# A gather stage with POOL fills in it, selections made for two groups at a time, and fewer waits on PE

## What is computed

```
def _gcn_conv(x, src, dst, ew, W, b, n_nodes):
    xW = x @ W
    deg = jax.ops.segment_sum(ew, dst, num_segments=n_nodes) + 1.0
    dinv = jnp.where(deg > 0, jax.lax.rsqrt(deg), 0.0)
    norm = dinv[src] * ew * dinv[dst]
    agg = jax.ops.segment_sum(norm[:, None] * xW[src], dst, num_segments=n_nodes)
    agg = agg + (dinv * dinv)[:, None] * xW
    return agg + b
...
h1 = jax.nn.relu(_gcn_conv(layernorm(x), ..., W1, b1, n))
h2 = jax.nn.relu(_gcn_conv(h1, ..., W2, b2, n))
x = x + h2
x = x + moe(layernorm(x))
```

## Time and profile before

| | |
|---|---|
| three runs, us | 5221.11, 5225.19, 5214.46 |
| the profiled execution, us | 5177.12, its span 5175.3 |
| first stage, up to POOL's first gather | 427 us |
| layer 1, POOL's first to last gather | 427 to 2677 us |
| layer 2, from POOL's first gather to the end | 2689 to 5175 us |
| busy shares of the span | PE 74%, weight loads 68%, POOL 58%, DVE 44%, ACT 14% |

### The profile page before, as it was taken

How to read it: one execution, slowest core, us unless ns; L and a number is a source line. 1 busy time by engine, 2 the same in 40 slices (tenths; PEclk the granted TensorE clock), 3 DMA queues, 4 the chain that set the end, 5 groups by cost and what they waited for, 6 DMA issues and landing times.

```text
span 5175.3 us, 82233 instructions
## 1 busy us (share of the span) xinstructions
PE 3841.7 (74%) x27222; PEld 3496.5 (68%) x27223; DVE 2298.3 (44%) x8827; ACT 722.4 (14%) x2277; POOL 3003.7 (58%) x3241
## 2 busy tenths in 40 slices
PE   3445565555555555555558999999999999999999
PEld 3424454554555545555557899889989899988998
DVE  6732222222222222222224655566556655656655
ACT  1020000000000000000001222222222222222222
POOL 0104666666666666666666666666666666656663
PEclk9998766766666666667668999999999999999999
DMA  3244333333333333333333333333333333333332
GB/s 95 62 144 122 99 97 97 100 96 98 98 97 100 96 97 99 95 98 98 97 94 93 95 97 99 96 96 96 96 98 96 96 97 98 96 93 95 95 97 59
DMA packets 243540, 500.39 MB, mean 97 GB/s; under 512 B 61453, under 2 KB 141656, under 8 KB 243179
## 3 DMA queue, kind: packets, MB, share of 16 engines
q0 software_dynamic: 150528, 411.24, 28.0%
q1 hardware_dynamic: 87210, 79.56, 4.9%
q10 hardware_dynamic: 5440, 5.01, 0.3%
HBM read 456.90 MB, written 38.67 MB: 96 GB/s over the span
## 4 chain that ended last, share of the span: by engine, by line
PE 28%; DVE 19%; POOL 18%; issue 16%; another core or an unknown queue 14%; DMA 3%; DVEq 2%; SPq 1%; ACT 0%; POOLq 0%; ACTq 0%
POOL msg L461 18%; PE part L736 11%; DVE sel L1047 5%; PE psY L730 5%; PE psH L721 3%; PE psY L736 3%; DVE mix L1175 2%; PE psH L736 2%; DMA msg<-ytab,srcT 1%; DVEq L272 1%; DVE accbuf L1055 1%; DVE accbuf L989 1%; DVE nt L1129 1%; PE psT L689 1%
## 5 line engine op out<-in xcount | busy, mean ns | idle before, releaser
L461 POOL DMA_INDIRECT msg<-ytab,srcT x3136 | 2968.1, 946 | 1878.2 <-issue 962.3
L736 PE MATMUL part<-sel,msg 128*128 128x96 f32 x8384 | 1155.9, 293 | 255.6 <-issue 207.9
L736 PEld LDWEIGHTS part<-sel,msg 128*128 128x128 f32 x8384 | 1113.6, 210 | 310.6 <-issue 270.1
L730 PE MATMUL psY<-w_s,hS 128*128 128x256 f32 x3136 | 838.1, 390 | 19.6 <-DVE mix L1175 10.1
L1047 DVE TENSOR_SCALAR sel<-iota,relT,ewT 128x96 f32<-128x96 f32 x3136 | 838.6, 342 | 2.5 <-ACT accbuf L514 1.6
L721 PEld LDWEIGHTS psH<-tokS,w_s 128*128 128x128 f32 x6272 | 811.3, 192 | 36.1 <-issue 0.5
L721 PE MATMUL psH<-tokS,w_s 128*128 128x128 f32 x6272 | 813.9, 275 | 0.4 <-issue 0.4
L1055 DVE TENSOR_TENSOR accbuf<-accbuf,part 128x192 f32 x524 | 185.6, 354 | 1215.8 <-remote 744.3
L553 ACT ACTIVATE hS<-psH,b_s 128x128 f32<-128x128 f32 x1568 | 487.7, 362 | 1411.9 <-PE psH L721 798.6
L730 PEld LDWEIGHTS psY<-w_s,hS 128*128 128x128 f32 x3136 | 543.3, 191 | 113.7 <-issue 64.3
L736 PE MATMUL psH<-sel,msg 128*128 128x96 f32 x2080 | 370.0, 335 | 251.4 <-issue 232.6
(11 more groups left out here) (167 smaller groups left out, 2024.8 us busy)
## 6 DMA issues: line engine op xcount, KB each, us to landing
msg<-ytab,srcT POOLq DMA_INDIRECT x3136
msg<-in_x SPq DMA_DIRECT2D x194, 128.0 KB, 2.1
ytab<-xS SPq DMA_DIRECT2D x99, 128.0 KB, 15.2
ytab<-msg SPq DMA_DIRECT2D x98, 128.0 KB, 1.7
xS<-in_x SPq DMA_DIRECT2D x98, 128.0 KB
out<-res SPq DMA_DIRECT2D x98, 128.0 KB
w_s<-in_L_ffn_w ACTq DMA_DIRECT2D x2, 2048.0 KB
accbuf<-in_dst SPq DMA_DIRECT2D x1, 588.0 KB
```

The source lines that it names most:

```text
L461: pool.indirect_dma_start(msg[:, r * GT + j, :], None, ytab[l], bass.IndirectOffsetOnAxis(ap=srcT[:, g * GT + j:g * GT + j + 1].bitcast(U3 ...
L730: mm = pe.matmul(psY[e % 2][:, 0:D], hS[:, e % 2, m, :], w2_s[:, e, m, :], start=(m == 0), stop=(m == KD - 1))
L736: m = pe.matmul(slot[:, h * W:(h + 1) * W], msg[:, tile0 + j, h * P:(h + 1) * P], sel[:, sel0 + j, :], start=(j == 0), stop=(j == GT - 1))
```

## The change

On POOL, behind the gathers of every third group of layer 1, two memsets of half of `hS` each are added (130 places, 260 memsets). Each waits for the one before it, on a new semaphore `s_rest`. ACT waits for all of them ahead of layer 2.

The 16 matmuls of a pair stand in one piece; in layer 2 PE's waits for messages and sums are the old ones. The diff, cut to its core:

```
+                if l == 0 and n % 3 == 2:
+                    for u in range(2):
+                        wait(pool, s_rest, n // 3 * 2 + u)
+                        pool.memset(hS[:, u, :, :], 0.0).then_inc(s_rest, 1)
...
+        act.wait_ge(s_rest, NG // 3 * 2)
...
-            wait(pe, s_linD[l], s.k - 1)
             if l == 1:
+                wait(pe, s_linD[l], s.k - 1)
                 wait(pe, s_bias, s.k - biases_behind)
...
             pe.wait_ge(s_y2, s.k)
-            wait(pe, s_y2C, s.k - 1)
...
-            if l == 0 and n % 2 == 0:
-                pe.wait_ge(s_msg[(q + 1) % MR], ((q + 1) // MR + 1) * (16 * GT))
-            pe.wait_ge(s_msg[m], (q // MR + 1) * (16 * GT))
-            pe.wait_ge(s_sel, q + 1)
+            if l == 1 or n % 2 == 0:
+                if l == 0:
+                    pe.wait_ge(s_msg[(q + 1) % MR], ((q + 1) // MR + 1) * (16 * GT))
+                pe.wait_ge(s_msg[m], (q // MR + 1) * (16 * GT))
+                pe.wait_ge(s_sel, q // 2 * 2 + 2)
             if l == 1:
                 pe.wait_ge(s_added, q - 1)
-            products(sums_of(l, n), m * GT, r * GT).then_inc(s_part, 1)
+            products(sums_of(l, n), m * GT, (r ^ 1) * GT).then_inc(s_part, 1)
...
         def selection(q):
             g, r = NG - 1 - q % NG, q % R
-            wait(v, s_part, q - R + 1)
-            for j in range(GT):
-                t = v.tensor_scalar(sel[:, r * GT + j, :], iota[:, 0:W], relT[:, g * GT + j:g * GT + j + 1],
-                                    ewT[:, g * GT + j:g * GT + j + 1], ALU.is_equal, ALU.mult)
-            t.then_inc(s_sel, 1)
+            tiles = slice((g - 1) * GT, (g + 1) * GT)
+            to = sel[:, r * GT:(r + 2) * GT, :]
+            wait(v, s_part, q - R + 2)
+            v.tensor_tensor(to, iota[:, 0:W].unsqueeze(1).broadcast_to([P, 2 * GT, W]),
+                            relT[:, tiles].unsqueeze(2).broadcast_to([P, 2 * GT, W]), ALU.is_equal).then_inc(s_sel, 1)
+            v.wait_ge(s_sel, q + 1)
+            v.tensor_tensor(to, to, ewT[:, tiles].unsqueeze(2).broadcast_to([P, 2 * GT, W]), ALU.mult).then_inc(s_sel, 1)
```

More of the change, by code:

```diff
@@ L267, in build @@
     s_out = sem("s_out")
+    s_rest = sem("s_rest")
     block = ctx.enter_context(nc.Block())
@@ L1208, in _ @@
         v.wait_ge(s_y1C, NB + XS)
-        for r in range(R):
+        for r in range(0, R, 2):
             selection(r)
@@ L1216, in _ @@
                 add(q, bases[R - 1 - r])
-                if q + R < NG:
-                    selection(q + R)
+                if r % 2 and q + R < NG:
+                    selection(q - 1 + R)
                 if s and r == 1:
@@ L1243, in turn @@
                     add(q, bases[R - 1 - r])
-                    if q + R < 2 * NG:
-                        selection(q + R)
+                    if r % 2 and q + R < 2 * NG:
+                        selection(q - 1 + R)
             turn(0)
```

## The result

| | before | after |
|---|---|---|
| median of the runs, us | 5217.78 (5214.46 to 5225.19, 4 runs) | 5306.01 (5305.69 to 5306.78, 4 runs) |
| ratio, 95% interval | | 1.0165 [1.0152, 1.0177] |
| profiled span, us | 5175.3 | 5304.2 |

The change makes the kernel 88 us slower, where 128 us less was forecast. The time lies in the range, and near the first rival's price of 5311, but not for that rival's reason, as the stages show. First the windows of the profile after, layer 1 and layer 2 from POOL's first gather on; they answer to the earlier trace rows.

A forecast was written before the change was run, and what follows sets the result against it. POOL was taken to pace layer 1, stopping for PE's held signals, and PE to bound layer 2. Stops -258 and breaks +130, other terms 0, gave 5221 - 128 = 5093 us; range 5025 to 5325.

The forecast's parts named there:

- first rival: Layer 1: POOL's breaks are paid in full and its stops stay; +90 us, 5311 us, chance 0.24.
- The stops, -258 us: Layer 1: breaks let PE's older signals through, so POOL's 100 stops of 2.9 us vanish; nine tenths of 285 us won.
- second rival: Layer 1: idle time is conserved as a nearly fixed share of the gathering, fills only shrink stops; 5221 us, chance 0.17.
- The breaks, +130: Layer 1, POOL: 130 breaks of two fills cost 1.0 us each beyond the ordinary gap; 130 us, between 81 and 159.
- PE's waits, 0: Layer 1, PE: four of six waits per 4 groups go, worth 0 us since POOL sets the pace.
- third rival: Layer 1: PE's signals come later since 32 records stand in one piece; 5727 us with the fills, chance 0.05.
- The selections' own time: DVE: two paired operations of 945 ns each, 2.0 us a pair with handover against 2 x 1.05 before; 0 us.
- cover of 0.4 us: Layer 1: the later selection, at 1526.1, is covered by PE's work on the pair in hand, up to 1526.5.
- fourth rival: Layer 1: gathers can't be issued during DVE's two-input operations, 372 us, partly replacing stops; +217 us, 5438 us, chance 0.04.
- Layer 2, 0 with a bound of +50: Layer 2: DVE's work ahead of the token stays about the same, 0 us, bounds -15 and +50 us.

The follow-up runs named there:

- e6: The kernel after, unchanged, run again with stops: 5310.91 us, 1.0166 of before.
- e17: Kernel before with two fills, four fills and paired selections in separate layer 1 stretches, turn 1's selection behind the token from layer 2's block 49; with stops, 5198.81 us beside 5223.92.
- e18: Kernel before with half of PE's products, half more of them, and a quarter of DVE's selections in separate layer 1 stretches; with stops, 5221.69 us beside 5216.68.
- e2: Kernel before with only the fills added, without stops: 4831.49 us, 1.0150 of before.
- e7: Kernel after with layer 2's selections made singly as before, with stops: 5228.68 us, 1.0010 of before.
- e1: Kernel before with only PE's waits changed, without stops: 4760.74 us, 1.0002 of before.
- e5: The kernel before, unchanged, run again for its trace, with stops: 5224.02 us.
- e3: Kernel before with only the paired selections, without stops: 4893.50 us, 1.0279 of before.
- e8: Kernel after with layer 2's paired selection of a block's second turn made behind the token, with stops: 5178.76 us, 0.9915 of before.
- e11: Kernel before with fewer PE waits, single selections and no fills in layer 1, and layer 2 as in e8; without stops, 0.9996 of before.

## Why the prediction was wrong, point by point

- **The stops, -258 us.** The failed step is "If every break lets the older signals through, the 100 stops of 2.9 us vanish". They shrank only by as much as the other parts added: from 328.5 us in 101 to 172.5 in 64 in e6, while POOL's busy time rose by 162.4. So a term of -258 against breaks of +130 came out, with the selections' part, at +7 us for the layer. Pauses, breaks and lengthening together are a fixed sum: that is the second rival, which stood at 0.17 for 5221 us. Its layer 1 is what e6 (+7 us), e17 and e18 show, but as a share of the gathers, not of the time a signal needs. Its own counter-argument, that no engine needs the time, was true and did not count (e18). The prediction took a regularity ("a pause of about 1 us if the run was 5 us long and 2 to 3 if it was 15 to 20") for a threshold that a pause has to pass; read as a ratio, the same rows gave the right answer, and the earlier trace rows could not tell these apart.
- **The breaks, +130.** The mechanism was right and the size was off: 0.55 us each, for no gap of 0.2 us stands around a fill. 130 of them are 71 us (e2), below the lowest bound of 81. With stops they cost nothing that e7's ten runs or e17 can tell.
- **PE's waits, 0.** Right without stops, where e1 is 1.0002; with stops they were not run alone, but they are in e7, which is 6 us from before. The third rival (5727) falls by e6 and e7, where 32 records stand in one piece and layer 1 is 7 us longer and not 376.
- **The selections' own time.** 953 and 959 ns against 945: right. That layer 1 doesn't feel them is right with stops (5.78 in both stretches), but not for the cover of 0.4 us that I worked out; POOL's pace is the cover, and without stops they cost 83 us.
- **The fourth rival** (gathers can't be issued during two-input operations) was right in part and its size too large: 83 us in layer 1 and not 372. A gather does start beside them and is lengthened by up to 0.8 us, as if it went on at the end of the operation it began under, and one that began before them mostly isn't lengthened. The lengthening takes the place of stops, as that rival said.
- **Layer 2, 0 with a bound of +50.** This is the step that made the kernel slower. I counted "2.0 us in one turn instead of 1.05 in each of two, about the same". The two turns are not alike: turn 1's selection stands between DVE's last wait and the token that PE waits for, and turn 0's is followed by a wait. Measured +83 us with stops (e6 against e7 and e5), +51 without (e3). The bound was half a microsecond a block; the trace says 0.9. DVE's timeline of one block of layer 2, which would have told it, is not among the rows.
- **The first rival** came near by its number, 5311 against 5306, by luck. That the time lies in the range is luck as well: a gain of 128 us did not come and a loss of 83 had been put at 0, and the range was wide enough for both. Its stops didn't stay; layer 1 moved by 7 us, and the loss is elsewhere.

## What to carry to other kernels

When work is merged from two places into one, look at each place for the wait ahead of it and the engine that waits behind it: the same operations cost 83 us in front of the token, and gave 50 behind it. Where a pause recurs with a fixed ratio to an engine's work, try first the reading that it is a share that has to be paid, and that whatever fills it is free and buys nothing. And where a kernel runs in one of two conditions, put the variants into stretches of one kernel and read each against its neighbours. e8 is worth 0.85% in the one condition; its layer 2 with a layer 1 without fills and pairs (e11) is neutral in the other. e8 itself was not run there, nor e11 with stops.

## What was not expected of the hardware

- The same program, the kernel before, took 5222 us in some sets of runs and 4756 in others. The gathers' own length in layer 1 is the same (949 and 951 ns in e5 and e1), the stops of 3.3 us are there throughout or not at all, and layer 2 differs by 162 us (2510.80 in e5 against 2348.50 in e1, which has no edit there) at a granted clock of 0.99 in both.
- In the slower one a gather of layer 1 takes 1.43 to 1.46 us of POOL's time with its idle time, with all that was tried beside it: fills, paired selections, half or one and a half times PE's products, a quarter of DVE's selections (e17, e18).
- A gather that runs beside a 0.95 us operation of DVE with two tensor inputs took up to 1.79 us, but 0.95 beside operations of 0.26 us with one tensor input and two scalars. In layer 1 of e3 the lengthened ones are those that begin under such an operation, and they end 0.82 us behind its end; one that began ahead of the pair mostly keeps its 0.95 us.
- Two fills of 256 columns take 0.70 us together, with a gap of 0.06 us between them in all 130 breaks of after, though the second waits for the first by a semaphore.
